# One store of seven PSUM banks with two or three places for scores, a rewritten weight preparation, and a refitted order

## The reference, cut to what matters

```python
x = x + 0.5 * ffn(layernorm(x))       # pass 0 in the kernel
x = x + attn(layernorm(x))            # passes 1 (q, k, v) and 2 (output projection)
x = x + 0.5 * ffn(layernorm(x))       # pass 3

def fp4_linear(x, w):                 # both sides rounded to an 8-value grid,
    return fp4(x) @ fp4(w).T          # one scale for each block of 16
def ffn(x):
    h = silu(fp4_linear(x, w_gate)) * fp4_linear(x, w_up)     # 256 -> 704
    return fp4_linear(h, w_down)                              # 704 -> 256
def attn(x):                          # 8 heads, each the difference of two softmaxes
    q, k = rope(rmsnorm(x @ Wq.T)), rope(rmsnorm(x @ Wk.T))   # 16 half-heads of 16
    p = softmax(causal(q @ k.T / 4))                          # 16 x 2048 x 2048
    o = (p[:, 0] - lam * p[:, 1]) @ v                         # v: 8 heads of 32
    return (layernorm(o) * (1 - 0.362)) @ Wproj.T
```

## Time and profile before

| | us |
|---|---|
| median of 3 runs | 2233.28 |
| lowest, highest | 2229.14, 2234.44 |
| the profiled execution | 2234.47 |
| its span | 2232.7 |
| PE, ACT, DVE, POOL busy | 1908.8, 1718.7, 1575.5, 1349.4 |

### The profile page before, as it was taken

How to read it: one execution, slowest core, us unless ns; L and a number is a source line. 1 busy time by engine, 2 the same in 40 slices (tenths; PEclk the granted TensorE clock), 3 DMA queues, 4 the chain that set the end, 5 groups by cost and what they waited for, 6 DMA issues and landing times. The chain is left out here.

```text
span 2232.7 us, 39312 instructions
## 1 busy us (share of the span) xinstructions
PE 1908.8 (85%) x13634; PEld 787.6 (35%) x13634; DVE 1575.5 (71%) x3333; ACT 1718.7 (77%) x2530; POOL 1349.4 (60%) x1427
## 2 busy tenths in 40 slices
PE   1677898898989889989989898899998889998865
PEld 1343443343423333434333343344333323432222
DVE  8888887787736778879645787777855678730464
ACT  3456788877888879678988898777888898889851
POOL 5797776566635676776645676676744556630353
PEclk9899999999999999999999999999999999999987
DMA  4133444224212354333312345322521334320112
GB/s 121 25 67 74 84 81 74 55 63 81 43 42 37 67 97 75 73 71 55 63 46 35 64 85 97 64 48 58 85 53 27 70 67 72 62 46 1 20 36 54
DMA packets 477492, 136.15 MB, mean 61 GB/s; under 512 B 458224, under 2 KB 477040, under 8 KB 477296
## 3 DMA queue, kind: packets, MB, share of 16 engines
q1 hardware_dynamic: 477296, 133.65, 32.1%
HBM read 11.96 MB, written 8.39 MB: 9 GB/s over the span
## 5 line engine op out<-in xcount | busy, mean ns | idle before, releaser
L996 ACT ACTIVATE probs<-psum_s 128x1024 f32<-128x1024 f32 (+3 forms) x1280 | 1074.3, 900 | 124.9 <-PE psum_s L1284 100.7
L1302 PE MATMUL psum_o<-probs,v_sb 128*32 128x512 f32 (+3 forms) x5120 | 576.5, 545 | 21.1 <-POOL probs L901 12.9
L1245 PE MATMUL shared<-w_gu_T,xT 128*128 128x512 f16 (+1 forms) x2304 | 517.1, 373 | 69.5 <-DMA xT<-x 21.3
L1284 PE MATMUL psum_s<-q_stack,k_stack 64*128 64x512 f16 (+3 forms) x2560 | 397.2, 354 | 111.6 <-ACT probs L996 102.6
L1245 PEld LDWEIGHTS shared<-w_gu_T,xT 128*128 128x128 f16 x2304 | 213.7, 100 | 347.5 <-issue 84.1
L1258 PE MATMUL shared<-w_down_T,hT 128*128 128x256 f16 x2176 | 273.1, 282 | 42.8 <-DMA hT<-h 28.1
L1284 PEld LDWEIGHTS psum_s<-q_stack,k_stack 64*128 64x128 f16 x2560 | 98.9, 93 | 542.1 <-ACT probs L996 446.4
L901 POOL TENSOR_SCALAR_AFFINE_SELECT probs<-probs 128x512 f32<-128x512 f32 x256 | 174.6, 686 | 165.9 <-ACT probs L996 165.0
L868 POOL TENSOR_TENSOR hq<-grid,qscale 128x704 f32<-128x704 f32 x128 | 182.7, 1428 | 142.2 <-DVE grid L1096 142.2
L835 POOL TENSOR_TENSOR hq<-hq,rscale 128x704 f32<-128x704 f32 x128 | 187.0, 1461 | 110.2 <-DVE rscale L1029 109.9
L1258 PEld LDWEIGHTS shared<-w_down_T,hT 128*128 128x128 f16 x2176 | 212.0, 101 | 109.3 <-issue 48.1
(11 more groups left out here) (119 smaller groups left out, 2341.9 us busy)
## 6 DMA issues: line engine op xcount, KB each, us to landing
xb<-L_attn_x SPq DMA_DIRECT2D x16, 512.0 KB, 4.2
out<-xb SPq DMA_DIRECT2D x16, 512.0 KB, 3.0
xT<-x SPq DMA_TRANSPOSE x128, 3.1
hT<-h SPq DMA_TRANSPOSE x128, 3.5
k_stack<-st SPq DMA_TRANSPOSE x64, 3.2
q_stack<-st SPq DMA_TRANSPOSE x64, 3.3
k_stack<-L_ffn_w_down SPq DMA_DIRECT2D x1, 704.0 KB, 4.1
k_stack<-L_ffn_w_gate SPq DMA_DIRECT2D x1, 512.0 KB, 5.2
```

Of the source, the lines that this page charges most:

```text
L996: nc.scalar.activation(probs[:, s % 3, 2 * u:2 * u + 2, q0:CHUNK], psum_s[u][:, :, q0:CHUNK], ACT.Exp, scale=HD ** -0.5 / QK_SCALE ** 2).t ...
L1245: last = nc.tensor.matmul(bank(e)[:, 0:hi - lo], xs[:, x, t % 2, k, :], w_gu_T[:, w, k, lo:hi], start=n == 0, stop=n == len(parts) - 1)
L1284: last = nc.tensor.matmul(psum_s[u][:, j, q0:CHUNK], k_stack[half, at, h, kt % NTC * P:(kt % NTC + 1) * P], q_stack[half, c % 2, h, q0:CHU ...
L1302: last = nc.tensor.matmul(psum_o[at:at + VD, q0:CHUNK], v_sb[:, kt // NTC % SLOTS * NTC + kt % NTC, 2 * g + u, :], probs[:, s % 3, 2 * u + ...
```

## The change

1. **PSUM.** `psum` is one tensor of seven banks beside `psum_o`. A `scores` stage takes two adjacent free banks, by preference those starting at 0, 2, 4, 5, 1, 3; all others take one bank, by preference 4 to 6, and at most three at once as before (`LOANS`). Two pairs of scores may be out at a time; in the turns of the table `WIDE` (356 of the 640 steps) three. A stage waits for the last user of its bank, whoever that was (`wait_bank`). The exps still run in their old order.
2. **Setup.** The product of `scaled_weights` goes from DVE to POOL, with a scale already multiplied by `SCALE_UP` (one more small DVE instruction each). `v_sb` is filled only in its last column of each head. `powers` shifts its bits within PSUM. The six tiny instructions become seven on POOL, the lambda products go to POOL, the scaling of `rope_sb` to ACT. Wv is transposed ahead of w_down. The attention maxima and the low halves of w_gate come ahead of chunk 0's grid stages.
3. **DUE** has all numbers new, so the whole order is another one.

```diff
-BANKS = 3
+BANKS = 7
+LOANS = 3
+NARROW_SCORES, WIDE_SCORES = 2, 3
+LONE = 4
+PAIRS = (0, 2, 4, 5, 1, 3)
+WIDE = {0: (2, 3, 4, 8, 13, 14, 15), 1: (3, 7, 11, 12, 14, 15), 2: (1, 3, 4, 5, 7, 11, 14, 15), 3: (0, 2, 3, 4, 6, 7, 11, 14, 15)}
...
-    "stats0": (-3774073, -2422530, ...
+    "stats0": (-4961561, -3404689, ...
...
+                if r == "scores":
+                    b = pairs[user] = next(b for b in PAIRS if max(free_bank[b:b + 2]) <= start)
+                    free_bank[b:b + 2] = [math.inf, math.inf]
...
-        psum_s = [ctx.enter_context(nc.psum_tensor(f"psum_s{u}", [P, 2, CHUNK], F32)) for u in range(2)]
-        shared = [ctx.enter_context(nc.psum_tensor(f"shared{i}", [P, 512], F32)) for i in range(BANKS)]
+        psum = ctx.enter_context(nc.psum_tensor("psum", [P, BANKS, CHUNK], F32))
...
+        def wait_bank(engine, e):
+            scored, freed = 0, {}
+            for user in plan.before[e]:
+                if user and user[0] == "scores":
+                    scored = max(scored, 2 * user[1] + user[2] + 1)
+                elif user:
+                    freed[BANK[user][0]] = BANK[user][1] + 1
...
-                    if s >= 1:
-                        pe.wait_ge(exp_done, 2 * s + u - 1)
...
-                    nc.gpsimd.memset(v_sb[:, :, :, :], 1.0).then_inc(fills_done, 1)
+                    nc.gpsimd.memset(v_sb[:, :, :, VD - 1:VD], 1.0).then_inc(fills_done, 1)
...
-                        wait(done(nc.vector.reciprocal(r, s)))
-                        nc.vector.scalar_tensor_tensor(w, w, TIE_DOWN, r.unsqueeze(2).broadcast_to([P, nb, QB]),
-                                                       ALU.mult, ALU.mult).then_inc(w_scaled, 1)
+                        wait(done(nc.vector.tensor_scalar(w_near[:, 0:nb], s, SCALE_UP, None, ALU.mult)))
+                        nc.vector.reciprocal(r, w_near[:, 0:nb]).then_inc(w_inverse, 1)
```

More of the change, by code:

```diff
@@ L262, in order @@
         self.ring = {r: {} for r in self.sizes}
-        banks = [[0, 0] for _ in range(BANKS)]
+        loans, free_bank, of_loan = [0] * LOANS, [0] * BANKS, {}
+        last_user, users, leads = [None] * BANKS, [0] * BANKS, 0
+        pairs = {}
         out = {e: [] for e in ENGINES}
@@ L280, in ready @@
                 if r == "bank":
-                    first = min(b[0] for b in banks)
+                    first = max(min(loans), min(free_bank))
                     if first == math.inf:
@@ L312, in order @@
                 if r == "bank":
-                    b = min(range(BANKS), key=lambda i: banks[i][0])
-                    self.bank[user] = (b, banks[b][1])
-                    banks[b] = [math.inf, banks[b][1] + 1]
+                    loan = min(range(LOANS), key=lambda i: loans[i])
+                    b = min(range(BANKS), key=lambda i: (free_bank[i] > start, i < LONE, free_bank[i]))
+                    loans[loan] = free_bank[b] = math.inf
+                    of_loan[user] = loan, b
+                    if name in LEAD:
+                        b, leads = leads % LEAD_BANKS, leads + 1
+                    self.bank[user] = b, users[b]
+                    users[b] += 1
+                    self.before[user] = [last_user[b]]
+                    last_user[b] = user
                 else:
                     self.ring[r].setdefault(user, len(self.ring[r]))
+                if r == "scores":
+                    b = pairs[user] = next(b for b in PAIRS if max(free_bank[b:b + 2]) <= start)
+                    free_bank[b:b + 2] = [math.inf, math.inf]
+                    self.before[name] = last_user[b:b + 2]
+                    last_user[b:b + 2] = [name, name]
             if name[0] in PORT and engine in held:
@@ L339, in order @@
                 if r == "bank":
-                    banks[self.bank[user][0]][0] = end[name] + REACH["tensor"]
-                else:
+                    loan, b = of_loan[user]
+                    loans[loan] = free_bank[b] = end[name] + REACH["tensor"]
+                else:
+                    if r == "scores":
+                        b = pairs[user]
+                        free_bank[b:b + 2] = [end[name] + RELEASE] * 2
                     freed[r][self.ring[r][user]] = end[name] + RELEASE
@@ L345, in order @@
         self.end = end
+        self.pairs = pairs
         self.left = left
@@ L682, in macaron_kernel @@
         assert not any(e in LEAD for engine in order for e in REST[engine])
+        assert all(plan.bank[e][0] < LEAD_BANKS for e in LEAD if e in plan.bank)
         first = {kind: [e for engine in order for e in FIRST_OF[engine] if e[0] == kind]
@@ L755, in bank @@
         def bank(e):
-            return shared[BANK[e][0]]
+            return psum[:, BANK[e][0], :]
         def full(e):
@@ L1415, in macaron_kernel @@
                     moves.append((4 if a == 3 else 3, [w_att[:, a, r, k * P:(k + 1) * P] for r in range(KC)], P, *to))
-            banks = [psum_s[0][:, 0], psum_s[0][:, 1], psum_s[1][:, 0], psum_s[1][:, 1]]
+            banks = [psum[:, b, :] for b in range(LEAD_BANKS, BANKS)]
             NB = len(banks)
```

194 lines of the change are left out of this document (114 added, 80 removed), and 136 rows, old and new, of the table DUE.

## The result

The changed kernel takes **2176.1 us** (median of four runs, 2174.0 to 2177.4); the kernel before, on the same chip, 2233.9. The ratio is 0.9738, with a 95% interval of 0.9720 to 0.9756: 58 us less. What happened is the rival "the gain is larger" (2174).

A forecast was written before the change was run, and what follows sets the result against it. DVE bounds the setup and ramp, an engine-changing chain the middle, ACT the end of attention, one chain the tail. Terms -9 - 14 - 14 + 13 = -24 on 2234.5 gave 2210.5, predicted as 2210 us, range 2180 to 2238.

The forecast's parts named there:

- Setup: Before the main block: 14.8 us leave DVE, 9 stay after POOL overlap and reach the end: -9, bounds 2 and 14.
- the gain is larger: Rival, middle: the refitted order takes the waits on both sides, middle gives -50, total 2174 us; chance 0.20.
- My walk: Setup: new instruction list stepped through with profiled durations; main block starts at about 55.6 instead of 64.6 us.
- my bound of 8.4 us: Setup: lower end of the gain, each POOL product blocking DVE for its whole length, 8.4 us lost.
- Middle: Main block, 240 to 2000 us: third place lets scores run with two exps owed; -14, bounds -81 and +7.
- the upper bound of 81: Middle: all waits of 40% of the stages gone on both sides, 0.40 x (100.7 + 102.6) = 81 us.
- End of attention: Turns (14, 1) to (14, 3): moved work shortens 82.9 us to 69; -14, bounds -6 and -17.
- Tail: After the last copy: moved work is done behind the last values, lengthening chunk 14's chain; +13, bounds +5 and +20.
- Slower: the borrowed banks starve the MLP: Rival: with three pairs out, hidden or down wait for exps and hold up PE's queue; 2249 us, chance 0.10.
- Only the setup gains: Rival: exp waits for other things instead, the two ends cancel; 2225 us, or 2230; chance 0.17.
- The setup gains nothing: Rival, setup: shared port makes DVE stand by, main block at 62, all else as forecast; 2217 us, chance 0.10.

The follow-up runs named there:

- the held order: Changed kernel, its order kept word for word, 501 scores stages also waiting for the exp two back (all 501 waits): 2247.1 us.
- those of chunks 13 to 15: Changed kernel, order kept, the added wait for the exp two back only in turns of chunks 13, 14 and 15 (182 waits): 2202.5 us.
- three neighbours: Changed kernel with DUE numbers shifted: by up to 200000, 2326.7 us; by up to 20000 in two patterns, 2314.9 and 2292.2 us.
- the first small pattern: Changed kernel with each due time in DUE moved by at most 20000, first of two patterns: 2314.9 us, ratio 1.0355.

## Why the prediction was right or wrong

**What bounds the kernel.** Right: DVE the setup, a chain over all engines the middle, ACT the end. Right too that the two ping-pong sums must not be added: the held order gave 71 us for 118 us of waits.

**Setup: the mechanism right, -5.75 instead of -9.** What leaves DVE left it. Three rows have their answers:

```profile
6.91 0.21 DVE L1621 TENSOR_SCALAR hq<-hq 128x96 f32<-128x96 f32 x1
...
31.47 0.16 DVE L1653 TENSOR_SCALAR hq<-psum_o 128x3 int32<-128x3 int32 x1
...
47.37 0.69 DVE L1685 TENSOR_REDUCE hq<-hq 128x16 f32<-128x512 f32 x1 [0.71 <-ACT hq L1753]
```

The first scale takes 0.21 where it took 2.69, the last of `powers` 0.16 where it took 2.73, and the 2.39 us wait for the Wv transposes is 0.71. The POOL products cost 2.8 each as taken. What I missed lies in two places: the grid stages of the weights are longer beside POOL's work, and DVE now waits for ACT. First DVE's timeline, then POOL's, then ACT's:

```profile
17.76 1.76 DVE L1631 SCALAR_TENSOR_TENSOR probs<-probs,k_stack 128x1536 f32<-128x1536 f32 x1
...
25.67 2.83 DVE L1631 SCALAR_TENSOR_TENSOR probs<-probs,k_stack 128x1536 f32<-128x1536 f32 x1 [0.47 <-ACT probs L1743]
28.53 2.50 DVE L1632 SCALAR_TENSOR_TENSOR k_stack<-probs 128x1536 f32<-128x1536 f32 x1
...
49.63 2.68 DVE L1607 SCALAR_TENSOR_TENSOR w_down_T<-psum,hq,w_down_T 128x256 f16<-128x256 f32 x6 [1.26 <-ACT w_down_T L1753]
54.45 1.66 DVE L1607 SCALAR_TENSOR_TENSOR w_qkv_T<-psum,hq,w_qkv_T 128x256 f16<-128x256 f32 x4 [2.15 <-ACT w_qkv_T L1753]
```

```profile
8.40 2.80 POOL L1531 TENSOR_TENSOR k_stack<-k_stack,hq 128x1536 f32<-128x1536 f32 x1 [2.71 <-DVE hq L1624]
...
21.32 5.56 POOL L1531 TENSOR_TENSOR k_stack<-k_stack,hq 128x1536 f32<-128x1536 f32 x2
26.85 5.10 POOL L888 TENSOR_TENSOR xq<-xq,rscale 128x512 f32<-128x512 f32 x2
```

```profile
29.45 0.60 ACT L977 ACTIVATE psum<-xq 128x512 f32<-128x512 f32 x1 [3.81 <-POOL xq L888]
31.98 0.60 ACT L977 ACTIVATE psum<-xq 128x512 f32<-128x512 f32 x1 [1.93 <-POOL xq L888]
```

The pair at 25.67 and 28.53, beside POOL's 5.10, takes 1.8 more than a clean one, where I had priced that overlap for DVE at 0.17. I had read only the first half of the pair in the trace of before: its second half (at 31.89, not shown) took 2.50 there too. A third pair beside another POOL stage loses another 1.1. And DVE had become fast enough to catch up with ACT: it waits 1.26 and 2.15 us for ACT's high halves, where I had it run through. My walk came out 3.3 us early. It put the start of `grid_points(1)` at 25.0 (25.7), the end of `powers(0)` at 30.1 (31.6), the end of `grid_points(2)` near 43 (44.6), the last low half near 54 (56.9) and the main block at 55.6 (58.9): the first half of the error is the overlap, the second the waits for ACT.

The rows above show how the two engines hold each other up: each waits until the other's instruction is done, then it is the other's turn. DVE's first product ends at 28.50, 1.6 us behind POOL's weight product at 26.88. POOL's next product, 1.1 us elsewhere, was due at 26.85 but is read by ACT at 29.45 only, so it ran behind DVE's. DVE's second product ends at 31.03, 1.6 behind that, and POOL's second is read at 31.98, 0.95 behind DVE's. The block maxima at 8.87 (1.75 us) beside POOL's product at 8.40 (2.80) show none of this; the scale instruction behind them shows it again, 0.62 instead of 0.21, ending with POOL's product (11.27 and 11.20).

The prediction left out a condition of the rule. In "SBUF — State Buffer" (SBUF: two separate sides) the Trainium skill names what takes the shared pair on VectorE's side: an instruction in a two-port mode, or one with two inputs in SBUF, and the latter only against a GpSimd instruction that reads SBUF. The trace agrees: the grid products have two such inputs and alternate with POOL's in whole instructions, and the block maxima, with one input, lost nothing. So my bound of 8.4 us, a POOL product's whole length lost each time, was drawn too wide: only a few DVE instructions are of the kind that waits, and beside the first product at 8.40 there was but the one scale.

That 9 us "pass to the end one for one" was the other half of this step. Alone, 5.4 us of earlier start were worth 5.0 at the last copy of the trace and 2 in the timed runs; in the changed order 5.7 were worth 9 in the trace and 11 (5 to 17) in the timed runs. Why the two orders differ is not shown.

**Middle: the failed step.** I put it as "I take 40% of ACT's waits alone, 40 us, and of that a third": -14, bounds -81 and +7. It was -40.5. The cause was right and the share was wrong: the slack at run time alone, with the order held, is worth 71 us over the whole program, of which 38 are in chunks 3, 7 and 11. I cut the sum to ACT's side without a reason (against the larger gain I held that PE works 90%), and to a third, since other things are late too. PE is a single queue in which `hidden`, `down` and `values` stand behind a waiting scores stage, so a wait of scores is paid by what stands behind it: `tanh` waits 17.8 us less for `hidden`, and the wait added back in the held order raised it again, from 80.7 to 100.0:

```profile
ACT hq L969 <- PE psum L1298: 100.0, 89, 4.2
```

The cut to ACT's side is thus what failed first: in the held order 86 of the 118 us of waits are on PE's side. That the upper bound of 81 lies near the 71 is luck, since it was built on 0.40 of 203 us of waits, while the slack takes away 118 us of waits, of which 71 reach the end. The second thing I had not seen is that the 71 us are not a distance to the kernel before. Its order is fitted to two places; the changed order without its slack is 13 us slower than it (2247.1 against 2233.9). At the end of turn (15, 3) the order without its slack stands at +21.7 and the changed kernel at -46.2, so 68 of the 75 us between the two traces are earned by then, and the rest of the change, the earlier start included, gives 22 of them back. I had treated the order as given and the place as the gain, while the runs show that they go together: the place with the old table costs 31 us, the order fitted to it without its slack 13. The planner's own sum for the two orders, 50 us apart, stood nearer to the measured 58 than my 24, and it needed no run.

**End of attention: the direction right, -19.3 instead of -14, beyond the bound of -17.** What I counted, the work moved out, is there. Two slips. ACT is busy 97% of it (61.96 of 63.6), and I took 93% from the turns before; its busy time itself is 2 us under the 64 that I had summed. The exps of that window:

```profile
L1048 ACT ACTIVATE probs<-psum 128x1024 f32<-128x1024 f32 (+3 forms) x71 | 58.3, 1005 | 1.5 <-PE psum L1333 1.4
```

Exps waited 5.9 us for scores there, now 1.4. I wrote that the third place has nothing to take where attention is alone. That was drawn from one run of fifteen exps and is false for these turns: with the old wait they are 7 us longer (all 501 waits, 2083.78 to 2154.59) or 10 (those of chunks 13 to 15). So a third to a half of the -19.3 is the place, and a part of the near hit is luck.

**Tail: right, +8.5 instead of +13.** The chain's marks, from the copy at 2079.45:

```profile
2104.20 1.41 DVE L1101 BATCH_NORM_STATS2 stat<-xb 128x6 f32<-128x256 f32 x4
...
2112.09 0.69 DVE L1075 TENSOR_REDUCE psum<-xq 128x32 f32<-128x512 f32 x1 [0.70 <-ACT xq L990]
...
2125.50 8.26 PE L1296 MATMUL psum<-w_gu_T,xT 128*128 128x512 f16 x30 [2.02 <-DMA xT<-x]
```

Stats come 24.75 us behind the copy, 18.15 before: +6.6 (forecast +8). To scale_x it is 7.9 instead of 6.15: +1.7 (+1). To `hidden` 13.4 instead of 12.7: +0.7 (+3). From there to the end 50.2 instead of 50.7. DVE's list up to stats holds what I had counted. Where the forecast is too high is behind it: the gate, the scale and the add between the two scale_x delay the first grid_x by 2.1 us (5.2 instead of 3.1 behind scale_x), and 1.4 of these are made good before `hidden`.

**The rivals.** "The gain is larger" is what happened, by the reason that stood for it (waits on both sides), and the reason against it (PE at 90% already) did not hold: PE works 91% of a middle window that is shorter (1545.53 of 1700). "Slower: the borrowed banks starve the MLP" is refuted by the waits of PE. The stages other than scores and values wait for an exp in four rows of the changed kernel, the largest being

```profile
PE psum L1309 <- ACT probs L1048: 0.6, 1, 0.6
```

and the sum 1.4 us, where 42 would have decided it. "Only the setup gains" falls with the held order. "The setup gains nothing", which had the main block start at 62, falls with the row at 58.89, though in the old order the timed runs show only 2 us of it.

**What stays open.** The old kernel with a table fitted anew was not run, so how much of the 58 us a better fit of the two fixed places would give isn't known. Nor was a search for a still better table around the changed kernel made; three neighbours are all far slower. The store of seven banks with two places was run with the new table only; with the old one the planner gives it the lists of the kernel before.

## What to carry to other kernels

A wait at the head of an in-order queue is paid by everything behind it, so price a removed wait on both engines of a ping-pong and start from the sum of both sides, not from one side's. To measure what a buffer is worth, hold the instruction order and put back only the wait; if a planner makes a new order with each edit, measure first how far a tiny shift of its numbers moves the time (here by 57 to 151 us), because any edit that reorders is judged against that, and read the planner's own sum of each order before the chip's. Before a mark in two programs is called progress, compare how many instructions each engine has done by then.

## What was not expected of the hardware

**The same matmuls took PE a different time.** All these programs have 13634 of them. The pages of the changed kernel, of the kernel before and of the first small pattern on the changed kernel:

```profile
PE 1884.4 (87%) x13634; PEld 782.7 (36%) x13634; DVE 1566.9 (72%) x3324; ACT 1710.4 (79%) x2531; POOL 1365.6 (63%) x1439
```

```profile
PE 1908.8 (85%) x13634; PEld 787.6 (35%) x13634; DVE 1575.5 (71%) x3333; ACT 1718.7 (77%) x2530; POOL 1349.4 (60%) x1427
```

```profile
PE 1927.0 (83%) x13634; PEld 792.8 (34%) x13634; DVE 1575.7 (68%) x3324; ACT 1719.5 (74%) x2531; POOL 1367.5 (59%) x1439
```

The mean granted clock was 0.975, 0.967 and 0.959 in the three. In the middle it is 0.99 for the changed kernel's window and 0.98 before. I had no term for this: PE's busy time alone is 24 us less after the change. In these three the matmuls take longer where the clock is lower, but that is not the whole of the difference: the run with all 501 waits has more idle time of PE and still 0.975, with PE busy 1896.8, and the one without a third place has the clock of the kernel before, 0.967, with PE busy 1923.5. What sets the two apart was not isolated.

**DVE and POOL side by side take turns, but only some instructions do.** In the setup DVE's products of two SBUF operands, 1.76 us alone, took 2.83 and 2.50 beside POOL's, and POOL's pair of 1.1 us products took 5.10, each ending one behind the other. A DVE reduction of 1.75 us beside a POOL product of 2.80 cost neither anything.
